# A planner's DMA delays set from a trace: a two-layer AdaLN kernel on one core

## The reference

```python
h = layernorm(x) * (1 + ca) + sa;  x = x + ga * L0_attention(h)   # 8 heads of 16
h = layernorm(x) * (1 + cb) + sb;  x = x + gb * L0_ffn(h)         # dense mixture of 8 experts, two weighted
h = layernorm(x) * (1 + ca) + sa;  x = x + ga * L1_mamba(h)       # scan over 512 tokens, 256 channels, 16 states
h = layernorm(x) * (1 + cb) + sb;  x = x + gb * L1_ffn(h)         # 8 experts of capacity 153, two per token
```

## Time and profile before

| | us |
|---|---|
| median of three runs | 3219.97 |
| the profiled execution | 3232.89 |
| its span, first to last instruction | 3231.7 |
| PE, DVE, ACT, POOL busy in the span | 2248.2, 2569.1, 1554.1, 1224.5 |
| mean granted TensorE clock, share of full speed | 0.818 |

### The profile page before, as it was taken

One profiled execution on the slowest core, in us unless ns is written; L12 is line 12 of the kernel. 1 busy time (PEld: TensorE's weight loads), 2 busy tenths in 40 slices (PEclk: granted clock), 3 DMA queues, 4 the chain that ended last, 5 costly groups with the idle time before them and its releaser, 6 DMA issues.

```text
span 3231.7 us, 34184 instructions
## 1 busy us (share of the span) xinstructions
PE 2248.2 (70%) x8658; PEld 1163.9 (36%) x8767; DVE 2569.1 (79%) x6529; ACT 1554.1 (48%) x3348; POOL 1224.5 (38%) x1118
## 2 busy tenths in 40 slices
PE   4068396877868687777768777777867778668644
PEld 2015132544234432444235522445325532345213
DVE  5974887889888898879888897979889897954482
ACT  3406633675256733676145843567236752534322
POOL 1020053623544154523544154532535144533461
PEclk8579597888978888878978788788979879779757
DMA  4011012232132312322133211323121421313222
GB/s 96 0 25 31 0 40 78 75 76 75 44 91 69 96 49 61 88 69 86 47 84 76 84 54 54 93 58 93 56 75 63 102 58 47 91 31 113 73 69 91
DMA packets 137464, 215.15 MB, mean 67 GB/s; under 512 B 17872, under 2 KB 57440, under 8 KB 134112
## 3 DMA queue, kind: packets, MB, share of 16 engines
q1 hardware_dynamic: 133088, 203.88, 23.0%
q0 software_dynamic: 4096, 8.40, 0.9%
HBM read 190.06 MB, written 22.15 MB: 66 GB/s over the span
## 4 chain that ended last, share of the span: by engine, by line
DVE 38%; PE 23%; issue 21%; POOL 6%; ACT 5%; DMA 2%; another core or an unknown queue 2%; DVEq 2%; SPq 1%; POOLq 0%; ACTq 0%
DVE wmask L765 13%; PE ps_att L1018 3%; DVE best L900 3%; PE ps_rest L1297 3%; PE ps_rest L1307 3%; DVE hg L1578 2%; DVE hfc L1566 2%; PE ps_att L1029 2%; POOL gat L1606 2%; DVEq L902 2%; PE ps_rest L1523 1%; PE ps_rest L1393 1%; DMA cols<-slots 1%; ACT wmask L747 1%
## 5 line engine op out<-in xcount | busy, mean ns | idle before, releaser
L765 DVE TENSOR_SCALAR_CACHE_REDUCE wmask<-z,tc 128x512 bf16<-128x512 f16 x640 | 438.8, 740 | 25.0 <-ACT z L732 22.8
L1367 POOL TENSOR_TENSOR gat<-sil,cbs 128x512 f32<-128x512 f32 x256 | 324.8, 1270 | 181.8 <-PE ps_rest L1297 114.2
L1332 ACT ACTIVATE sil<-ps_rest,w_b1T 128x512 f32<-128x512 f32 x256 | 175.7, 687 | 443.5 <-PE ps_rest L1307 424.0
L1018 PE MATMUL ps_att<-z,Vp 128*32 128x128 f32 x2048 | 290.8, 291 | 42.6 <-DVE z L1090 27.6
L934 POOL TENSOR_SCALAR wmask<-wmask 128x512 bf16<-128x512 bf16 x256 | 162.4, 634 | 381.3 <-DVE wmask L891 375.2
L1619 POOL TENSOR_TENSOR rest_c<-rest_c,hg 128x512 f32<-128x512 f32 x128 | 162.5, 1269 | 362.2 <-DVE hg L1578 362.2
L1307 PE MATMUL ps_rest<-rest_hT,WF 128*128 128x512 f32 x512 | 286.3, 646 | 7.4 <-ACT sil L1332 7.3
L1297 PE MATMUL ps_rest<-gat,WP 128*128 128x512 f32 x512 | 273.2, 617 | 6.5 <-POOL gat L1367 5.6
L1018 PEld LDWEIGHTS ps_att<-z,Vp 128*32 128x32 f32 x2048 | 213.9, 116 | 141.4 <-issue 120.6
L1523 PE MATMUL ps_rest<-hg,ident 128*128 128x512 f32 x256 | 184.1, 809 | 115.0 <-DVE hg L1578 114.8
L1068 DVE CUSTOM_DVE_ANT_0 z<-ps_att,wmask 128x512 f32<-128x512 f32 x256 | 174.9, 683 | 105.5 <-PE ps_att L1006 80.1
(11 more groups left out here) (347 smaller groups left out, 5025.7 us busy)
## 6 DMA issues: line engine op xcount, KB each, us to landing
cbs<-spreads SPq DMA_DIRECT2D x128, 256.0 KB, 3.7
ccs<-spreads SPq DMA_DIRECT2D x128, 256.0 KB, 3.4
WF<-in_w SPq DMA_DIRECT2D x64, 256.0 KB, 2.6
WP<-in_w SPq DMA_DIRECT2D x64, 256.0 KB, 2.7
WF<-in_wfc SPq DMA_DIRECT2D x64, 256.0 KB, 2.6
WG<-in_wgate SPq DMA_DIRECT2D x64, 256.0 KB, 2.9
WP<-in_wproj SPq DMA_DIRECT2D x64, 256.0 KB, 3.3
qk<-bounce SPq DMA_DIRECT2D x32, 384.0 KB, 5.7
```

The lines of the kernel that those rows point to most:

```text
L765: od.up(dve.tensor_scalar(wmask[:, i, :], z_at[i], tc[:, 0, i:i + 1], None, ALU.is_ge, ALU.add, accum_out=tc[:, 1, i:i + 1]))
L1018: mm = pe.matmul(obank[o:o + 32, a * P:(a + 1) * P], Vp[:, kc, h, :], pT[u][:, kc, :], start=kc == 0, stop=kc == NT - 1)
L1367: weighed0.up(pool.tensor_tensor(gat[m % 2], sil[m % 2], cbs[e % 2][:], ALU.mult))
```

## The change

Signals can now have a list of lags, used in turn by the position of the signal's increment in its group. `stacked` gets fourteen: 4.2 to 9.8 us for the 11 loads of K and Q, 4.2 to 5.9 us for the 3 later ones, where all had 6.0. Seven other DMA signals get a number of their own: `outB` 1.3, `spreadB` 3.3, `spreadC` 3.1, `sent_in` 1.3, `slotted` 4.0, `stored` 2.9, `fetched` 1.6, where all had 2.8. `bounced` stays at 3.5.

```diff
     def __init__(self, sem, per, unit, lag, fresh):
-        self.sem, self.per, self.unit, self.lag = sem, per, unit, lag
+        self.sem, self.per, self.unit, self.lags = sem, per, unit, lag if isinstance(lag, tuple) else (lag,)
         self.when, self.fresh = [], fresh
...
+    def reached(self, end):
+        self.when.append(end + self.lags[len(self.when) % len(self.lags)])
...
-    splitted, bounced, stacked = sig("splitted", 3), sig("bounced", 9, 16, 3.5), sig("stacked", 14, 16, 6.0)
+    splitted, bounced, stacked = sig("splitted", 3), sig("bounced", 9, 16, 3.5), sig("stacked", 14, 16, (4.2, 5.2, 6.2, 6.7, 7.2, 7.7, 8.3, 8.7, 9.2, 9.6, 9.8, 4.2, 5.2, 5.9))
...
-    keptB, outB, spreadB, spreadC = sig("keptB"), sig("outB", 1, 16), [sig(f"spreadB{i}", NS // 4, 16) for i in range(4)], [sig(f"spreadC{i}", (NS + 2 - i) // 3, 16) for i in range(3)]
+    keptB, outB, spreadB, spreadC = sig("keptB"), sig("outB", 1, 16, 1.3), [sig(f"spreadB{i}", NS // 4, 16, 3.3) for i in range(4)], [sig(f"spreadC{i}", (NS + 2 - i) // 3, 16, 3.1) for i in range(3)]
...
-    picked1, counts1, shares, routed, sent_in, slotted = sig("picked1"), sig("counts1"), sig("shares"), sig("routed", 2), sig("sent_in", PICKS, 16), sig("slotted", 1, 16)
+    picked1, counts1, shares, routed, sent_in, slotted = sig("picked1"), sig("counts1"), sig("shares"), sig("routed", 2), sig("sent_in", PICKS, 16, 1.3), sig("slotted", 1, 16, 4.0)
...
-    res_ps, res_rows, stored, fetched = sig("res_ps", 3), sig("res_rows", 3), sig("stored", 1, 16), sig("fetched", PICKS, 16)
+    res_ps, res_rows, stored, fetched = sig("res_ps", 3), sig("res_rows", 3), sig("stored", 1, 16, 2.9), sig("fetched", PICKS, 16, 1.6)
...
             for one in fresh:
-                one.when.append(start + one.lag)
+                one.reached(start)
```

More of the change, by code:

```diff
@@ L2063, in weave @@
         for one in fresh:
-            one.when.append(one.lag)
+            one.reached(0.0)
         fresh.clear()
```

## The result

The changed kernel takes 3199.54 us, the median of 7 runs (3199.23 to 3207.49), the kernel before 3222.21 us (7 runs, 3207.39 to 3225.11). The ratio is 0.9933 with a 95% interval of 0.9915 to 0.9951, so 22 us less (16 to 27). The profile after is of a run of 3202.08 us.

The account below looks back on a forecast made before the run. DVE was taken to bound the period, with 43.6 us idle in it. Terms -3 + 2 + 1 + 0 = 0 left the profiled execution at 3232.89 us, 12.9 above the median, so the forecast was 3220.0, range 3206 to 3234.

Parts of the forecast that it names:

- A: Batch 0's seam: mixture norms move into DVE's gaps of 5.01 and 4.37 us; -3 us, bounds -9.4 and +1.9.
- No instruction is added or removed, no wait either, so every price is a shift: Whole kernel: the premise that the change only shifts existing work and waits; no size of its own.
- faster: both gaps stay filled: Rival: the 9.4 us of A go through to the end, B and C hidden by slack; 3210.6 us, chance 0.27.
- the end gets what lies between the two: Step in A: the two chains share DVE, gaining up to 3.9 and 1 to 2 us; the end gains 3.
- B: Seam into `experts0(1)`: PE turns routing weights before the experts' result, starting it later; +2 us, bounds 0 and +4.4.
- C: Finishes: batch 3's rows land later, L1844 steps of batches 2 and 3 move up; +1 us, bounds 0 and +3.6.
- D: The rest: steps of Q's preparation move later on DVE, one on POOL; 0 us, bounds -2 and +2.
- The gap as the load's: Batch 0's seam: DVE's 5.01 us wait goes back to PE's 5.40 us wait for a load of `qk`.

Follow-up runs that it names:

- w56: Kernel before with new lags for Q's eight loads in batches 5 and 6 only, moving two PE waits and no instruction; 0.9978, -7 us.
- s_b1: Kernel before with the new lags of `stacked` for batch 1's group only; 0.9950, -16 us.
- q_8: Kernel before with the eight lags of batch 1's Q loads at 8.0, the rest of `stacked` at 6.0; 0.9950, -16 us.
- b_again: Second profile of the kernel before's order, with the changed kernel's bookkeeping and all old lags; 3223.97 us.
- w6: Kernel before with new lags for Q's eight loads in batch 6 only, moving one PE wait and no instruction; 0.9985, -5 us.
- k7: Kernel before with new lags for batch 7's three rescaled K loads only; 0.9995, -1.6 us.
- k_b4: Kernel before with new lags for batch 4's three rescaled K loads only; 0.9986, -4.5 us.
- k_lags: Kernel before with the new lags of `stacked` in every batch but batch 1; 0.9951, -16 us.
- sb1w56: Kernel before with new lags of `stacked` in batch 1 and for Q's eight loads in batches 5 and 6; 0.9934, -21 us.
- only_stacked: Kernel before with only the new lag list of `stacked`, the seven other signals at 2.8; 0.9927, -23.5 us.
- only_others: Kernel before with only the seven other signals' new lags, `stacked` at 6.0; 1.0001, 0 us.
- b_pad16: Order of the kernel before with 16 more statistics (5.23 us of DVE) at the head of batch 0's first norm; 1.0011, +3.5 us.
- best1: Changed kernel with 12.0 instead of 6.7 to 9.8 for batch 4's Q loads; 0.9936 of the kernel before, -21 us.
- short36: Kernel before with Q's eight lags at 3.0 in batches 2 to 7, moving three PE waits further up and no instruction; 1.0080, +26 us.

## Why the prediction was wrong

Two steps failed: a term that was left out, and the size of A.

**"No instruction is added or removed, no wait either, so every price is a shift"** is the first step that failed. The waits are the same in number, but some of them move, and what I had written of the change ("The lag changes no wait", "each keeps its waits") is wrong. I had compared the order of instructions and taken each wait to go with the instruction behind it. The stall of 5.94 us at L1099 was in the trace of before, released by `qk<-bounce`, a transfer that L1099 doesn't use. Term missing: -7 us by w56.

**A, batch 0's seam, -3 with a bound of -9.4**, is the second. The mechanism was right (the gaps shrank to 2.24 and 1.76, as said) and the size was not: s_b1 and q_8 gave -16 (-22 to -10), beyond even the bound. So my rival "faster: both gaps stay filled" (3210.6) was the nearer one. What the traces show of these 16 us is less than half. The table counts from the start of L1121 of attention 0; the order of before up to attention 2 is in seven kernels (before, b_again, w6, w56, k7, k_b4, k_lags), the filled seam in four with nothing else new up to there (s_b1, q_8, sb1w56, only_stacked).

| | order of before | seam filled |
|---|---|---|
| batch 1's fourth count ends (L775) | 79.8 to 80.7 | 82.6 to 84.1 |
| batch 0's experts0 starts (L1310) | 95.9 to 96.8 | 90.3 to 91.8 |
| batch 1's search ends (L784) | 113.9 to 115.0 | 111.4 to 113.5 |
| batch 1's softmax starts (L1009) | 236.0 to 237.7 | 233.0 to 234.1 |
| attention 1 ends | 348.4 to 355.6 | 347.3 to 351.8 |
| attention 2 ends | 715.5 to 720.8 | 708.8 to 713.8 |

At the seam my two gains were nearly right: the experts start 5 us earlier (I had 3.9), the search ends 2 us earlier (1 to 2), though it is 3 us behind at its fourth count. What failed is the step behind that, that the end gets what lies between the two: by attention 2 the traces are 7 us apart in the mean. From there on they show no further gain: s_b1 and q_8 take 2493 us from attention 2 to the end, kernels with before's order 2488 to 2495. But the executions traced of s_b1 and q_8 are each the slowest of six, 8 to 9 us over their medians. So the rest of the 16 lies in executions that no trace shows, and its cause stays open. A higher clock is no explanation by these traces. In s_b1's the stretch before attention 2 ends (scan and softmax beside each other) has a higher granted clock than in b_again's, but k7, with before's order there, has nearly that clock too. Windows of b_again, then of s_b1, then of k7, at the same places in the program:

```profile
900.00:950.00 50.00, 30.79 (x121) 18.12 (x123) 42.66 (x67) 22.87 (x48) 28.18 (x18) 0.66 0.37 106
950.00:1000.00 50.00, 41.31 (x228) 25.68 (x231) 45.76 (x88) 34.34 (x82) 27.93 (x21) 0.90 0.24 75
1000.00:1035.00 35.00, 28.96 (x158) 18.09 (x159) 28.59 (x58) 17.07 (x39) 13.62 (x11) 0.90 0.43 83
```

```profile
891.00:940.00 49.00, 29.74 (x115) 16.91 (x115) 42.94 (x68) 22.47 (x47) 27.76 (x18) 0.71 0.42 116
940.00:989.00 49.00, 40.59 (x233) 26.08 (x236) 45.60 (x88) 34.52 (x82) 28.88 (x22) 0.93 0.26 78
989.00:1023.00 34.00, 28.29 (x159) 17.79 (x161) 29.73 (x58) 17.82 (x41) 13.30 (x11) 0.95 0.44 86
```

```profile
896.00:946.00 50.00, 29.70 (x115) 17.15 (x115) 42.74 (x66) 21.80 (x46) 27.05 (x18) 0.69 0.38 111
946.00:996.00 50.00, 41.32 (x233) 26.01 (x235) 45.66 (x88) 34.47 (x83) 28.83 (x22) 0.90 0.23 76
996.00:1030.00 34.00, 28.50 (x159) 17.91 (x162) 29.65 (x58) 17.96 (x42) 13.18 (x12) 0.95 0.43 86
```

0.66, 0.90 and 0.90 of the full clock in b_again, 0.71, 0.93 and 0.95 in s_b1, 0.69, 0.90 and 0.95 in k7. Single profiles differ by this much whatever the order at the seam.

**B, +2.** Nothing moved at this seam's end: the bound of 0 was right, for another reason than the one I gave (A). I had L1775 at 760 since the weights stood at 759.06 before. But the steps that move ahead of the last L1838 on DVE are the routing's own, which make the weights: I had counted them as a delay of the experts and left the weights where they were. only_others shows it without the filled gaps (its batch 0 split ends at 406.9):

```profile
750.79 1.06 PE L1207 MATMUL ps_rest<-ident,sm_c 128*8 128x128 f32 x4
751.64 2.19 PE L1775 MATMUL ps_rest<-ident,cols 128*128 128x128 f32 x10
```

Neither waits there; the last copy is done at 754.5, the split at 758.0.

**C, +1.** The place was right (0.51 us of wait at batch 3's statistics) and it is worth nothing: only_others holds B and C and is at 0 (-5 to +5).

**D, 0.** The reorders at the softmax of batches 4 and 7 were in it. They are worth -4.5 (-9 to 0) and -1.6 (-6 to +3), beyond the bound of -2 that I gave D, if the first is real.

**The gap as the load's** held: PE still waits for `qk<-bounce` up to 320.71, and b_pad16 put 5.23 us into DVE's gap for 3.5 (-1 to +8). The Trainium skill (DMA: Bandwidth & Descriptors, "Anatomy of one DMA — SWDGE (gpsimd) path") gives a fixed part of about 2 us and the bytes at 436 GB/s for one DMA on another issuing path. Eight loads issued 0.46 us apart don't follow it here: in before, those of batch 1 landed 7.1 to 10.2 us after issue, those of batch 6 6.5 to 9.4, where the fit would give 2.3, an estimate by that page. It matters for the missed term: the last load of batch 6, issued at 2134.73, landed at 2144.1 and so held L1099, whose `z` was there at 2138.87.

The measured terms are -16, -7, -4.5, -1.6 and 0, or -29 with an error of some 11, for -22 measured. Of the two largest effects the forecast had one at a fifth of its size and left the other out.

## What to carry to other kernels

Where a planner writes the engines' lists, its belief about a transfer decides where the engine's wait for it stands, and an engine that waits in order holds everything behind that wait. So compare the lists with their waits in them, and look in the trace for a wait whose releaser the waiting instruction doesn't use. A belief that is too short costs a stall; one that is too long cost nothing here (best1's 12.0 for loads that take 10).

## What the runs showed of the hardware

A stall of PE of 6 us cost more than its length: the products right behind it ran at half of the full clock in each of four such stalls read here (attention 5 in before, attention 6 and both L1533 places in short36). For the four products of L1099 that adds 1.8 us to the 6 (3.78 us instead of 1.98). In k_b4's stall of that kind the granted clock stood at 0.50 from 2133 to 2138 us, the lower of its two levels (1.2 GHz of 2.4), after PE had been idle from 2128.3 to 2135.0:

```profile
2133.00:2138.00 5.00, 2.96 (x4) 1.41 (x5) 0.00 (x0) 0.00 (x0) 0.00 (x0) 0.50 0.02 3
```

Executions of one kernel on one core scatter by 10 us of 3220 (before: 3207 to 3237 over all runs), so a change of 7 us needs a dozen runs: w56's 12 against 23 of before leave an interval of 5 us to either side.
